# Row maximum subtracted on the Vector engine, mask written by four 64x64 tiles, reciprocal roots seeded on the Scalar engine, and a new order of the slots

## What is computed

```
q = l2norm(q) * qs ; k = l2norm(k) * ksc           # l2norm(t) = t / max(|t|, 1e-12)
q = q * cos * scale + rotate_half(q) * sin * scale  # k likewise, with 1/scale
sim = einsum('bhwie,bhwje->bhwij', bq, bk2) * QK_SCALE
sim = where(mask, -finfo.max, sim)                  # window of 32, look one block back
attn = softmax(sim, -1)
out = einsum('bhwij,bhwje->bhwie', attn, bv2)
xn = (x - mu) / sqrt(var + 1e-05) * g + bln         # feed-forward: a * gelu(gate) @ W2
```

## Time and profile before

| | before |
|---|---|
| median of 3 runs | 3859.58 us |
| the profiled execution | 3861.25 us |
| its span, first to last instruction | 3859.4 us |
| TensorE granted clock, mean of the span | 0.981 |
| DVE busy | 3084.9 us (80%) |
| ACT busy | 2813.7 us (73%) |
| POOL busy | 2593.1 us (67%) |

### The profile page before, as it was taken

How to read it: one execution, slowest core, us unless ns; L and a number is a source line. 1 busy time by engine, 2 the same in 40 slices (tenths; PEclk the granted TensorE clock), 3 DMA queues, 4 the chain that set the end, 5 groups by cost and what they waited for, 6 DMA issues and landing times.

```text
span 3859.4 us, 114529 instructions
## 1 busy us (share of the span) xinstructions
PE 3768.1 (98%) x45088; PEld 2814.4 (73%) x45088; DVE 3084.9 (80%) x5893; ACT 2813.7 (73%) x5420; POOL 2593.1 (67%) x2328
## 2 busy tenths in 40 slices
PE   6999889999999999999999999999999999999998
PEld 4777547777777777777777777777777777777776
DVE  3343488888888888888888888888888888888885
ACT  2788357777777777777777777777777777777775
POOL 0233377777777777777777777777777777776772
PEclk8899799999999999999999999999999999999999
DMA  0000122212211121211221121211211121121111
GB/s 33 1 0 1 52 53 49 52 36 57 51 49 46 41 61 47 51 37 50 49 61 45 37 52 49 52 47 43 54 49 49 38 58 47 47 60 41 47 47 38
DMA packets 61804, 171.33 MB, mean 44 GB/s; under 512 B 9504, under 2 KB 21632, under 8 KB 60928
## 3 DMA queue, kind: packets, MB, share of 16 engines
q1 hardware_dynamic: 61312, 164.53, 16.8%
HBM read 21.89 MB, written 4.19 MB: 7 GB/s over the span
## 4 chain that ended last, share of the span: by engine, by line
PE 78%; DVE 6%; ACT 2%; issue 1%; POOL 1%; DMA 0%; SPq 0%; DVEq 0%; POOLq 0%; ACTq 0%
PE bank L830 11%; PE bank L761 9%; PE bank L811 9%; PE bank L846 9%; PE bank L712 7%; PE bank L782 6%; PE bank L714 6%; PE bank L713 6%; PE bank L1136 4%; PE bank L1149 3%; PE bank L797 3%; PE bank L776 2%; DVE mbuf L965 2%; DVE ss L946 2%; PE bank L1093 2%; DVE mbuf L966 2%
## 5 line engine op out<-in xcount | busy, mean ns | idle before, releaser
L1043 POOL TENSOR_TENSOR rotbuf<-mbuf 128x512 f32<-128x512 f32 x768 | 969.4, 1272 | 577.7 <-PE bank L761 473.5
L1057 POOL TENSOR_TENSOR rotbuf<-rotbuf,rs 128x512 f32<-128x512 f32 x768 | 789.7, 1044 | 103.1 <-DVE rs L139 95.7
L1067 POOL TENSOR_TENSOR probs<-probs,rden 128x768 f32<-128x768 f32 x384 | 564.8, 1471 | 189.4 <-DVE rden L1009 189.4
L946 DVE TENSOR_REDUCE ss<-sq 128x8 f32<-128x512 f32 x768 | 517.6, 674 | 108.5 <-ACT sq L870 108.3
L870 ACT ACTIVATE sq<-bank 128x512 f32<-128x512 f32 x768 | 459.1, 598 | 180.0 <-PE bank L714 173.6
L965 DVE TENSOR_TENSOR mbuf<-bank,table 128x512 f32<-128x512 f32 x768 | 527.5, 687 | 17.0
L966 DVE TENSOR_TENSOR mbuf<-bank,table 128x512 f32<-128x512 f32 x768 | 521.4, 679 | 0.0
L996 DVE TENSOR_REDUCE nmax<-bank 128x8 bf16<-128x768 f32 x384 | 364.3, 949 | 157.2 <-PE bank L782 157.2
L761 PE MATMUL bank<-ident,rotbuf 128*128 128x128 f32 x3072 | 456.7, 276 | 6.1 <-POOL rotbuf L1057 4.6
L712 PE MATMUL bank<-weights,inputs 128*128 128x512 bf16 x1152 | 443.4, 385 | 18.8 <-DVE mbuf L966 13.6
L830 PEld LDWEIGHTS bank<-probs_t,vbuf 96*64 96x64 f32 x12288 | 389.3, 138 | 77.5 <-issue 64.9
(11 more groups left out here) (106 smaller groups left out, 6751.5 us busy)
## 6 DMA issues: line engine op xcount, KB each, us to landing
vbuf<-v_stage SPq DMA_DIRECT2D x192, 384.0 KB, 4.5
vbuf<-v_stage SPq DMA_DIRECT2D x192, 256.0 KB, 4.2
vbuf<-v_stage SPq DMA_DIRECT2D x96, 128.0 KB, 4.5
stage<-in_wqkv SPq DMA_DIRECT2D x36, 256.0 KB, 5.5
weights<-in_wo SPq DMA_DIRECT2D x6, 512.0 KB, 6.6
weights<-in_x_t SPq DMA_DIRECT2D x1, 2048.0 KB, 7.5
out_t<-weights SPq DMA_DIRECT2D x1, 2048.0 KB, 8.3
weights<-out_t SPq DMA_DIRECT2D x1, 2048.0 KB, 11.0
```

What stands on the lines that cost most here:

```text
L946: e.tensor_reduce(b.ss[:, col:col + 8], b.sq[:, u % 2, :].rearrange("p (h d) -> p h d", h=8), AX_X, ALU.add).then_inc(s.sq_summed, 1)
L1043: e.tensor_tensor(b.rot[:, u, :], b.m1[:, u % 2, :], b.m2[:, u % 2, :], ALU.add).then_inc(s.rotated, 1)
L1057: e.tensor_tensor(v, v, r, ALU.mult).then_inc(s.scaled, 1)
L1067: e.tensor_tensor(probs, probs, b.rden[:, p % 2, :].unsqueeze(2).broadcast_to([P, 8, BLOCK_K]), ALU.mult).then_inc(s.probs, 1)
```

## The change

Five things are changed in the deep layers; the first attention and the layer norms stay as they are.

- The row maximum is no longer added by PE. `dve_max_of` keeps it in float32, and a new `dve_shift` subtracts it from the scores in the banks and writes the result to SBUF (128x768, one for each pair). `act_exp_of` takes the exponential in place in SBUF. The next pair's mask now waits for `dve_shift`, not for the exponential.
- The mask of a pair is written by four matmuls on the 64x64 tiles that the scores use, not by two on the whole array. A sixth mask table is loaded for it.
- The 11 instructions of `dve_newton` become one clamp on DVE, a logarithm and an exponential on ACT (`act_seed`), and one Newton step of three instructions on DVE (`dve_refine`).
- After the third Gelu of a slot ACT loads a function table that holds both logarithm and exponential; this takes the place of the load in front of the exponential.
- All slot lists and `WORK_RING` are in a new order.

```diff
 def pe_scores_of(e, s, b, at, ahead, p):
...
-    e.wait_ge(s.exps, k.c[4] + p)
+    e.wait_ge(s.shifted, k.c[4] + p)
...
-    mask = b.maskb[:, 2 + t, :].unsqueeze(1).broadcast_to([P, 4, BLOCK_K])
-    for parity in range(2):
-        e.matmul(b.scores[parity][:, 0:4 * BLOCK_K].rearrange("p (h k) -> p h k", h=4), b.identb[:, :], mask,
+    for blk_half, parity in ((0, 0), (1, 1), (0, 1), (1, 0)):
+        r, c = slice(64 * parity, 64 * parity + 64), slice(64 * blk_half, 64 * blk_half + 64)
+        kind = 2 if blk_half == parity else 4
+        mask = b.maskb[r, kind + t, :].unsqueeze(1).broadcast_to([64, 4, BLOCK_K])
+        e.matmul(b.scores[parity][c, 0:4 * BLOCK_K].rearrange("p (h k) -> p h k", h=4), b.identb[r, r], mask,
                  start=True, stop=False, skip_group_check=True)
...
-def pe_shift(e, s, b, at, ahead, p):
...
-    for parity in range(2):
-        shift = b.nmax[:, p % 2, 4 * parity:4 * parity + 4].unsqueeze(2).broadcast_to([P, 4, BLOCK_K])
-        mm = e.matmul(b.scores[parity][:, 0:4 * BLOCK_K].rearrange("p (h k) -> p h k", h=4), b.identb[:, :], shift,
-                      start=False, stop=True, skip_group_check=True)
-    mm.then_inc(s.shifted, 1)
...
 def act_exp_of(e, s, b, at, ahead, p):
...
-    e.wait_ge(s.pt_full, k.c[4] + (p - 1))
-    e.activation(b.deep_probs[:, p % 2, :, :].rearrange("p (b h) k -> p b (h k)", b=2), b.score_pair, ACT.Exp).then_inc(s.exps, 1)
+    probs = b.deep_probs[:, p % 2, :, :]
+    e.activation(probs, probs, ACT.Exp).then_inc(s.exps, 1)
...
+def dve_clamp(e, s, b, at, ahead):
...
+    e.wait_ge(s.newton, k.c[REFINE_OPS])
+    e.tensor_scalar(b.nx[:, :], b.ss[:, :], 1e-24, None, ALU.max).then_inc(s.clamped, 1)
...
+def act_seed(e, s, b, at, ahead):
...
+    e.wait_ge(s.clamped, k.c[1] + 1)
+    e.activation(b.na[:, :], b.nx[:, :], ACT.Ln).then_inc(s.logged, 1)
...
+    e.activation(b.rs[:, :], b.na[:, :], ACT.Exp, scale=-0.5).then_inc(s.seeded, 1)
...
+def dve_refine(e, s, b, at, ahead):
...
+    e.wait_ge(s.seeded, k.c[1] + 1)
+    e.tensor_tensor(a, y, y, ALU.mult).then_inc(s.newton, 1)
...
+    e.scalar_tensor_tensor(a, a, -0.5, x, ALU.mult, ALU.mult).then_inc(s.newton, 1)
...
+    e.scalar_tensor_tensor(y, a, 1.5, y, ALU.add, ALU.mult).then_inc(s.newton, 1)
...
+def dve_shift(e, s, b, at, ahead, p):
...
+    e.wait_ge(s.row_max, k.c[4] + (p + 1))
+    e.wait_ge(s.pt_full, k.c[4] + (p - 1))
+    e.tensor_tensor(b.deep_probs[:, p % 2, :, :].rearrange("p (b h) k -> p b h k", b=2),
+                    b.score_pair.rearrange("p b (h k) -> p b h k", h=4),
+                    b.dmax[:, p % 2, :].rearrange("p (b h) -> p b h", b=2).unsqueeze(3).broadcast_to([P, 2, 4, BLOCK_K]),
+                    ALU.subtract).then_inc(s.shifted, 1)
...
 def act_ff_gelu(e, s, b, at, ahead, c):
...
+    if c == NF - 1:
+        e.preload_act_table_set(EXP_SET)
```

More of the change, by code:

```diff
@@ L783, in pe_scores_of @@
                           b.q[r, slot, BLOCK_Q * blk:BLOCK_Q * (blk + 1)],
[L784 removed]
+                          b.k[r, k.par, slot, BLOCK_Q * blk:BLOCK_Q * blk + BLOCK_K], start=False, stop=j == 3,
                           skip_group_check=True)
     mm.then_inc(s.scores, 1)
[L789 to L799 removed]
 def pe_transpose_probs_of(e, s, b, at, ahead, p):
@@ L975, in dve_newton @@
         return
[L976 to L979, removed]
-            if k.m <= INSTANCES:
-                e.wait_ge(s.scaled, k.c[8])
-            if ff.ok:
-                e.wait_ge(s.ff_var_kept, ff.c[1] + 1)
-                e.wait_ge(s.ff_rstd, ff.c[1])
-        e.wait_ge(s.newton, k.c[NEWTON_OPS] + i)
-        rsqrt_op(e, i, b.nx[:, :], b.rs[:, :], b.na[:, :], b.ss[:, :], 1e-24, 1.0).then_inc(s.newton, 1)
+    if k.ok:
+        e.wait_ge(s.sq_summed, k.c[8] + 8)
+    if ff.ok:
+        e.wait_ge(s.ff_var_kept, ff.c[1] + 1)
+    e.wait_ge(s.newton, k.c[REFINE_OPS])
+    e.tensor_scalar(b.nx[:, :], b.ss[:, :], 1e-24, None, ALU.max).then_inc(s.clamped, 1)
+def act_seed(e, s, b, at, ahead):
+    k, ff = at(ahead), at(ahead - NORM_LAG)
+    if not (k.ok or ff.ok):
+        return
+    e.wait_ge(s.clamped, k.c[1] + 1)
+    e.activation(b.na[:, :], b.nx[:, :], ACT.Ln).then_inc(s.logged, 1)
+    if k.m <= INSTANCES:
+        e.wait_ge(s.scaled, k.c[8])
+    if ff.ok:
+        e.wait_ge(s.ff_rstd, ff.c[1])
+    e.wait_ge(s.logged, k.c[1] + 1)
+    e.activation(b.rs[:, :], b.na[:, :], ACT.Exp, scale=-0.5).then_inc(s.seeded, 1)
+def dve_refine(e, s, b, at, ahead):
+    k, ff = at(ahead), at(ahead - NORM_LAG)
+    if not (k.ok or ff.ok):
+        return
+    x, y, a = b.nx[:, :], b.rs[:, :], b.na[:, :]
+    e.wait_ge(s.seeded, k.c[1] + 1)
+    e.tensor_tensor(a, y, y, ALU.mult).then_inc(s.newton, 1)
+    e.wait_ge(s.newton, k.c[REFINE_OPS] + 1)
+    e.scalar_tensor_tensor(a, a, -0.5, x, ALU.mult, ALU.mult).then_inc(s.newton, 1)
+    e.wait_ge(s.newton, k.c[REFINE_OPS] + 2)
+    e.scalar_tensor_tensor(y, a, 1.5, y, ALU.add, ALU.mult).then_inc(s.newton, 1)
 def dve_max_of(e, s, b, at, ahead, p):
@@ L1384, in pe_deep_slot @@
+    pe_project_in(e, s, b, at, 2, 1)
+    pe_values_of(e, s, b, at, -1, 3)
+    pe_transpose_probs_of(e, s, b, at, 0, 0)
     pe_transpose(e, s, b, at, 1, 0)
     pe_transpose(e, s, b, at, 1, 1)
-def act_deep_slot(e, s, b, at):
+    pe_ff_rstd(e, s, b, at, -2)
+    pe_transpose(e, s, b, at, 1, 2)
+    pe_ff_down(e, s, b, at, -3)
+    pe_transpose(e, s, b, at, 1, 3)
+    pe_project_in(e, s, b, at, 2, 2)
+    pe_transpose_probs_of(e, s, b, at, 0, 1)
+    pe_scores_of(e, s, b, at, 0, 3)
+    pe_values_in(e, s, b, at, 2, 0)
@@ new lines, in pe_deep_slot @@
+    pe_project_in(e, s, b, at, 2, 3)
+    pe_transpose(e, s, b, at, 1, 4)
+    pe_project_out(e, s, b, at, -1)
+    pe_transpose(e, s, b, at, 1, 5)
+    pe_project_in(e, s, b, at, 2, 4)
+def act_deep_slot(e, s, b, at):
+    act_square(e, s, b, at, 0, 6)
+    act_copy_pt_of(e, s, b, at, -2, 2)
+    act_ff_square(e, s, b, at, -3)
+    act_square(e, s, b, at, 0, 7)
+    act_exp_of(e, s, b, at, -1, 0)
+    act_copy_out(e, s, b, at, -2, 1)
+    act_copy_t(e, s, b, at, -1, 6)
+    act_copy_v(e, s, b, at, 0, 1)
+    act_copy_pt_of(e, s, b, at, -2, 3)
+    act_copy_t(e, s, b, at, -1, 7)
@@ L1875, in constants @@
             masks[rows, 2 + t] = np.where(ok, 0.0, big)
+            masks[64 - 64 * half:128 - 64 * half, 4 + t] = masks[rows, 2 + t]
     half = np.arange(0, DIM_HEAD, 2, dtype=f)
```

199 lines of the change are left out of this document (93 added, 106 removed), and 8 rows, old and new, of the table WORK_RING.

## The result

| | before | after |
|---|---|---|
| median (4 runs each, side by side) | 3859.99 us | 3708.53 us |
| range | 3849.73 to 3878.95 | 3695.15 to 3712.96 |
| the profiled execution | 3861.25 us | 3708.4 us |
| its span | 3859.4 us | 3706.5 us |
| granted clock, mean of the span | 0.981 | 0.972 |

The changed kernel takes 0.9592 of the time (interval 0.9547 to 0.9638), 4.1% less. The forecast was 3680 us in 3635 to 3765: right in sign and range, 28.5 us too low.

What follows compares the result with a forecast made beforehand. The prediction took PE's list to bound the kernel: per slot, shift -1.36, mask -0.80 and wait +0.3 gave -1.86 us. Over 96 slots that is 179 us off 3861.25, forecast 3680 us, range 3635 to 3765.

Steps and rivals of the forecast that it cites:

- PE bounds the kernel; its list sets the slot.: Deep layers: PE lacks 0.07 us in a 34.33 us slot, which shortens by what leaves PE's list, start to start.
- The shift, -1.36: Adding the row maximum leaves PE: two matmuls of 0.34 us, four times a slot, -1.36 us.
- The mask, -0.80: Mask matmuls on quarter tiles take 0.22 us instead of 0.42, four times a slot: -0.80 us.
- the PE list of 32.2 us: PE's work per slot after the change: 34.33 less 1.36 for the shift and 0.80 for the mask.
- The wait at `pe_transpose(0, 7)`, 0.3: PE's second transpose of pieces 6 and 7 waits for DVE's products: chain 12.4 against 12.0 us, 0.3 us a slot.
- The subtraction, 0.95 us and not held by POOL: Subtracting the maximum on DVE, four times a slot: 0.95 us each, free of POOL contention, +3.6 us for DVE.
- The rival with held subtractions: POOL holds each DVE subtraction by 0.97 us, slot 35.4 us, time 3963 us, slower; chance 0.04.
- The roots, 1.3 us and -3.1: Root instructions on DVE fall from 4.7 to 1.6 us a slot, -3.1 us; the small roots at one step about 1.3.
- DVE 31.2 of 32.2 us, busy for 95%, waits near 1 us: DVE as second bound: 31.2 us of work a slot, busy 95% or more, waits near 1 us.
- DVE becomes the bound: Rival: DVE's 31.2 us plus waits of 1.7 for ACT and 0.4 for PE, slot 33.3 us, about 3760 us; chance 0.17.
- Fill and drain as they are: Pipeline fill and drain stay unchanged, so the saving is 96 slots x 1.86 = 179 us.

Runs made afterwards that it cites:

- b_seed: Kernel before with the new roots alone (seed by logarithm and exponential on ACT, one clamp and one refinement on DVE), old order: 3857.61 us, ratio 1.0009.
- a_l7up0: a_load7 with the first up product moved ahead of scores 0, so values 0 follow them directly: 3658.57 us, ratio 0.946; repeated on another chip 3677.8 us, 0.9473.
- a_load7: Changed kernel with the second table load of a slot moved behind the squares of pieces 6 and 7: 3693.05 us, ratio 0.9539.
- a_newton: Changed kernel with the 11 old root instructions back on DVE and no seed on ACT: 4077.63 us, ratio 1.0516.
- b_mask4: Kernel before with only the new mask, four matmuls on 64x64 tiles: 3850.82 us, ratio 0.9937.

## Why the prediction was right, and where its sizes were off

- **PE bounds the kernel; its list sets the slot.** Right. PE lacks 0.99 us in 1000, and the steps on PE add up to the slot's change. That DVE's share does not matter by itself, b_seed shows.
- **The shift, -1.36.** Measured -1.32.
- **The mask, -0.80.** Right to the digit, but by luck: three sizes were off and cancel. The matmuls take 0.19, not 0.22, the scores behind them 0.76, not 0.82, and the step in front is 0.09 us longer. The Trainium skill, "TensorEngine Tiling (Array Packing)", Key Properties, says that a change of the tiling mode drains TensorE. The trace agrees for the change from the whole array to tiles: of the 0.09 us in front of the mask, 0.06 was inside the scores before. For the change from the scores' 64x64 tiles to the values' 96x64 it shows nothing: the scores take 0.76 us there too (a_l7up0).
- **What this left out.** The term that failed is the PE list of 32.2 us: it took all other steps as unchanged. The new order has eight entries into tiles a slot in place of seven (one values product no longer stands behind scores), which is 0.09 us, and two more ways out of tiles into float32 groups on balance, 0.2 us; with two smaller steps that is the +0.22 us of the table, and PE's list without its wait is 32.4 us, not 32.2. The prediction had the new order in view and counted only what was removed. a_l7up0 shows the cause for one entry and one way out, by undoing them: -0.19 us. For the other steps it is read from the timeline and was not tested by a run.
- **The wait at `pe_transpose(0, 7)`, 0.3.** The place and the cause were right, shown by a_load7; the size is 0.2. The chain of spans was 12.4 against 12.0 us, and neighbours overlap.
- **The subtraction, 0.95 us and not held by POOL.** Right: 955 ns on the mean over 242. The rival with held subtractions is refuted. It reads a bank and one SBUF table; the small root instruction with both inputs in SBUF (L1006) lasted 1153 ns on the mean beside POOL, its two followers 228. The Trainium skill, "SBUF — State Buffer", on the shared port pair, says that a DVE instruction with two SBUF inputs contends with GpSimd's reads, and that one with at most one SBUF input, outside the two-port modes, does not. The trace agrees with that here (955 against 1153 ns). But the count of SBUF inputs alone, by which the prediction went, is not enough: in a_newton the seed instruction L134, with a single SBUF input of int32, took 1177 ns where L139 beside it took 228, and in a_load7 the clamp L979, also with one, took 660 ns on the mean where it takes 189 in the changed kernel. In which mode they ran, no run shows.
- **The roots, 1.3 us and -3.1.** The step is 0.19 + 1.15 + 0.23 + 0.23 = 1.8 us of spans. The prediction took the means of before, 553, 544 and 234 ns, in which one in three of L138 and L139 was held and hardly any of L136; in the changed kernel the first instruction, L1006 in L136's place, is held in every slot. a_newton gives 2.9 us for the whole.
- **DVE 31.2 of 32.2 us, busy for 95%, waits near 1 us.** Occupied 32.61 - 1.6 = 31.0 us, busy for 93%, waits 1.6. "DVE becomes the bound" did not happen, but it was close: with the roots on DVE (33.9 us) it did, at 36.49 us a slot. The rival's rule, occupied time and 2.1 us of waits, would give 36.0 there, so its price was about right; the measured waits were 2.6.
- **Fill and drain as they are.** This is half of the miss. The forecast for the profiled run was 3682, measured were 3708.4. Slots: 179 forecast, 163.8 measured and 0.9 at the end, so 14 us. The rest is the first norm's start, 596.0 where it was 584.2, 12 us, in code that hardly changed.

These 12 us go with the granted clock. Busy times and clock of two stretches in which the first attention runs, in the kernel before:

```profile
100.00:150.00 50.00, 49.45 (x633) 37.05 (x629) 16.94 (x61) 36.29 (x163) 13.23 (x16) 0.79 0.01 2
150.00:200.00 50.00, 48.71 (x775) 36.94 (x774) 19.87 (x70) 44.87 (x203) 16.54 (x20) 1.00 0.00 0
```

and in the changed kernel:

```profile
100.00:150.00 50.00, 50.00 (x447) 37.39 (x445) 11.41 (x42) 26.21 (x118) 9.92 (x12) 0.50 0.01 2
150.00:200.00 50.00, 49.24 (x659) 37.22 (x659) 17.59 (x63) 36.69 (x164) 13.72 (x17) 0.82 0.00 0
```

The granted clock is the column with 0.79 and 1.00 (0.50 is the level of 1.2 GHz). In the changed kernel TensorE stayed at 1.2 GHz to past 150 us, though from 100 to 150 it was busy for all of the 50 us, and did 447 matmuls there where before it did 633. This is no property of the change: the first norm starts at 596.0, 609.3 us in two executions of the changed kernel, at 585.2 and 612.5 in two of a_l7up0, and at 580.9 in b_seed and 622.8 in b_mask4, which ran on one chip and have the same code up to there. The two of a_l7up0 part in this way too: from 300 to 400 us the clock is 1.00 in one and 0.76 in the other, with PE busy for 97.6 and 98.7 us. What decides it was not found.

## What to carry to other kernels

When PE is full, price an edit as its list from start to start, and beside the instructions removed count in the new order the entries into quarter or half tiles (0.09 us each here) and the ways out of them into a float32 group (0.10; into a bf16 projection about nothing). Parts of a change are not additive: shift and mask with the old roots and order cost 9%, the new roots alone gave nothing, and all of it in the new order gave 4%, so price the second bound with all parts in. When an instruction moves to another engine, its waits move with it, and what is queued behind it there matters more than its own length.
